# Two transformer layers on one core: the table that fixes every engine's order is laid out in stretches, with eight weightings of TensorE's kinds of jobs tried for each

## What is computed

```python
x = x + attn0(layernorm(x))   # one head, keys and values of 64, causal, with biases
x = x + ffn0(layernorm(x))    # x and weight rounded to fp8, fp16 product, plus bias
x = x + attn1(layernorm(x))   # 16 heads of 16, rotary positions, causal, output projection
x = x + ffn1(layernorm(x))    # mixes each row with the row before it, then
                              # sigmoid(xr @ W_r.T) * (square(relu(xk @ W_k.T)) @ W_v.T)
```

## Time and profile before

| what | value |
|---|---|
| median of three executions | 2672.41 us |
| the profiled execution's own time | 2668.14 us |
| its span, first to last instruction | 2666.3 us |
| TensorE matmuls (PE) busy | 2458.1 us, 92% |
| VectorE (DVE) busy | 1994.6 us, 75% |
| ScalarE (ACT) busy | 1555.9 us, 58% |
| GpSimd (POOL) busy | 597.0 us, 22% |
| mean granted TensorE clock | 0.973 |
| DMA | 159.33 MB, mean 60 GB/s |

### The profile page before, as it was taken

The page is one execution under the profiler, slowest core; times in us unless marked ns, Lnnn a source line. Parts: engine busy times, 40 slices in busy tenths (PEclk is TensorE's granted clock), DMA queues, the critical chain, the costliest instruction groups (busy, mean ns, idle before and its releaser), DMA issues.

```text
span 2666.3 us, 57570 instructions
## 1 busy us (share of the span) xinstructions
PE 2458.1 (92%) x21618; PEld 1123.5 (42%) x21618; DVE 1994.6 (75%) x4256; ACT 1555.9 (58%) x2785; POOL 597.0 (22%) x584
## 2 busy tenths in 40 slices
PE   6888799999999999999999999999989999999996
PEld 4544233444444343453443534343344533433344
DVE  4768788887867878777877778878776788797812
ACT  2335366665645666665655656656655567676662
POOL 5563120213043030222204213030313300000011
PEclk8999799999999999999999999999999999999998
DMA  2323231212212122030302313012130222111110
GB/s 61 103 83 97 67 84 29 67 50 57 78 37 81 49 72 73 26 107 22 96 26 65 97 43 95 20 49 80 40 89 25 72 60 65 39 52 38 29 42 26
DMA packets 225600, 159.33 MB, mean 60 GB/s; under 512 B 91824, under 2 KB 225072, under 8 KB 225328
## 3 DMA queue, kind: packets, MB, share of 16 engines
q1 hardware_dynamic: 224560, 154.75, 20.7%
q10 hardware_dynamic: 768, 0.92, 0.1%
HBM read 87.36 MB, written 67.63 MB: 58 GB/s over the span
## 4 chain that ended last, share of the span: by engine, by line
PE 62%; DVE 21%; ACT 6%; issue 4%; SPq 3%; DMA 1%; POOL 1%; DVEq 1%; POOLq 0%; ACTq 0%
DVE mx L1424 13%; PE psum L1726 13%; PE psum L1703 12%; PE psum L1674 6%; PE psum L1640 4%; ACT probs L1198 3%; PE psum L1514 2%; PE psum L1757 2%; PE psum L1604 2%; PE psum L1575 2%; PE psum L1765 2%; PE psum L1777 2%; PE psum L1746 2%; PE psum L1661 2%; SPq L854 2%
## 5 line engine op out<-in xcount | busy, mean ns | idle before, releaser
L1198 ACT ACTIVATE probs<-psum 128x512 f32<-128x512 f32 x2176 | 1143.8, 605 | 594.6 <-PE psum L1703 380.8
L1424 DVE TENSOR_REDUCE mx<-psum 128x1 f32<-128x512 f32 (+2 forms) x2304 | 1288.6, 623 | 221.4 <-PE psum L1674 165.7
L1703 PE MATMUL psum<-qst,kst 34*128 34x512 bf16 (+7 forms) x5120 | 665.9, 350 | 61.1 <-ACT probs L1198 24.1
L1726 PE MATMUL psum<-probs,vs 128*17 128x512 f32 (+3 forms) x5120 | 585.3, 539 | 0.4
L1674 PE MATMUL psum<-kst,qst 64*128 64x512 bf16 (+3 forms) x2560 | 435.7, 353 | 59.8 <-DVE mx L1424 21.9
L1703 PEld LDWEIGHTS psum<-qst,kst 64*128 64x128 bf16 (+1 forms) x5120 | 190.9, 94 | 412.4 <-ACT probs L1198 134.0
L1674 PEld LDWEIGHTS psum<-kst,qst 64*128 64x128 bf16 x2560 | 132.2, 94 | 371.6 <-ACT probs L1198 136.0
L1726 PEld LDWEIGHTS psum<-probs,vs 128*17 128x17 f32 x5120 | 93.2, 96 | 182.8 <-issue 154.0
L992 POOL TENSOR_SCALAR vare<-mv 128x4 f32<-128x4 f32 x64 | 15.3, 240 | 631.0 <-DVE mv L1300 631.0
L1681 PE MATMUL psum<-maskq,identh 64*128 64x64 bf16 (+1 forms) x2048 | 126.8, 204 | 0.0
L1148 ACT ACTIVATE probs<-psum 128x1024 f32<-128x1024 f32 x80 | 74.6, 940 | 83.3 <-PE psum L1581 49.4
(11 more groups left out here) (160 smaller groups left out, 2847.2 us busy)
## 6 DMA issues: line engine op xcount, KB each, us to landing
qk_dram<-parts SPq DMA_DIRECT2D x224, 128.0 KB
qst<-qk_dram SPq DMA_DIRECT2D x384, 64.0 KB, 2.1
kst<-qk_dram SPq DMA_DIRECT2D x384, 64.0 KB, 2.0
v_dram<-vst SPq DMA_DIRECT2D x64, 136.0 KB, 3.9
vs<-v_dram SPq DMA_DIRECT2D x64, 136.0 KB, 2.2
xs<-x_in SPq DMA_DIRECT2D x16, 512.0 KB, 3.9
x_dram<-xs SPq DMA_DIRECT2D x16, 512.0 KB, 2.9
att_dram<-ast SPq DMA_DIRECT2D x64, 128.0 KB, 2.0
```

The lines of the kernel that those rows point to most:

```text
L1198: act.activation(dst, src, ACT.Exp, scale=DK1 ** -0.5).then_inc(S["exp"], 1)
L1424: ins = dve.tensor_reduce(mx1[:, n % 2, 2 * g + odd, tile % TPC, c:c + 1], bank(src, at, at + cols), AX.X, ALU.max)
L1703: ins = pe.matmul(two[odd][:, at:at + cols], kst[rows, kslot, part, pair, keys], qst[rows, qslot, part, pair, CH - cols:CH], start=(part = ...
L1726: ins = pe.matmul(bank(7, off, CH, rows=VW, row=32 * h), vtile[:, h, :], probs[:, HG * (step_no(b, hg, k) % 2) + h, at:at + CH - off], sta ...
```

## The change

Keys, assumed durations, job lists and everything that builds instructions stay as they are. Only the way in which `run` picks the order changes. It now works in stretches of 40 (assumed us). At the start of each stretch it copies the state and follows eight ways for two stretches (80): way 0 has no weights, the other seven add to the key of every TensorE job a random weight between -10 and +10 that depends on its kind (turn, max, scores, values and so on; the random numbers are seeded, so that the table is the same each time). The way with the least TensorE time that isn't work (waiting and changes of mode) at the end of the two stretches wins, the real state is taken one stretch further with it, and the next eight are tried from there. The sets of jobs and of instructions are the same, in another order, and the banks are dealt out anew. Since the file grows by 51 lines above the instructions, L1674 is L1725 in the changed kernel, L1703 is L1754, and so on.

```diff
@@ -188,12 +188,41 @@
 PATIENCE = 0.25
 
+STRETCH, WAYS, MOVE = 40.0, 8, 10.0
...
+class State:
+    def __init__(self, left, listed, jobs):
...
+        self.now, self.mode, self.todo, self.work = 0.0, None, len(listed), 0.0
+
+    def copy(self):
...
@@ -225,19 +254,39 @@
-        todo = len(self.listed)
...
+        state = State(left, self.listed, jobs)
+        at = 0
+        while state.todo:
+            best = None
+            for way in range(WAYS):
+                weights = self.weights(at, way)
+                trial = state.copy()
+                self.go(trial, then, number, (at + 2) * STRETCH, weights)
+                rank = (max(trial.free_at["PE"], (at + 2) * STRETCH) - trial.work, way)
+                if best is None or rank < best[0]:
+                    best = (rank, weights)
+            at += 1
+            self.go(state, then, number, at * STRETCH, best[1])
+
+    def weights(self, at, way):
+        kinds = sorted({name[0] for name in self.listed if self.jobs[name][0] == "PE"})
+        if way == 0:
+            return {}
+        by = np.random.RandomState(WAYS * at + way).uniform(-MOVE, MOVE, len(kinds))
+        return dict(zip(kinds, by))
...
-        while todo:
+        while todo and now < until:
...
-                    rank = (jobs[name][1] - (STICK if jobs[name][7] == mode and e == "PE" else 0.0), number[name])
+                    rank = (jobs[name][1] - (STICK if jobs[name][7] == mode and e == "PE" else 0.0) + weights.get(name[0], 0.0),
+                            number[name])
...
                 start = now
+                if e == "PE":
+                    state.work += time
```

More of the change, by code:

```diff
@@ L196 @@
 scored, paired = [], []
+class State:
+    def __init__(self, left, listed, jobs):
+        self.left = left
+        self.ready = {e: [] for e in ("PE", "DVE", "ACT", "POOL", "SP")}
+        for name in listed:
+            if not left[name]:
+                self.ready[jobs[name][0]].append(name)
+        self.ready_at = dict.fromkeys(listed, 0.0)
+        self.free_at = dict.fromkeys(self.ready, 0.0)
+        self.order = {e: [] for e in self.ready}
+        self.vacant = [0.0] * 8
+        self.home, self.tenants, self.start = {}, {}, {}
+        self.now, self.mode, self.todo, self.work = 0.0, None, len(listed), 0.0
+    def copy(self):
+        new = State({}, (), {})
+        new.now, new.mode, new.todo, new.work = self.now, self.mode, self.todo, self.work
+        new.left, new.ready_at, new.free_at = dict(self.left), dict(self.ready_at), dict(self.free_at)
+        new.home, new.start, new.vacant = dict(self.home), dict(self.start), list(self.vacant)
+        new.ready = {e: list(names) for e, names in self.ready.items()}
+        new.order = {e: list(names) for e, names in self.order.items()}
+        new.tenants = {n: list(names) for n, names in self.tenants.items()}
+        return new
 class Order:
@@ L227, in run, with go @@
                 then.setdefault(a, []).append(name)
-        ready = {e: [] for e in ("PE", "DVE", "ACT", "POOL", "SP")}
         number = {name: n for n, name in enumerate(self.listed)}
[L230 to L240, removed]
+        state = State(left, self.listed, jobs)
[11 more added lines that the diff above has]
+            self.go(state, then, number, at * STRETCH, best[1])
+        self.home, self.tenants, self.total, self.start = state.home, state.tenants, max(state.free_at.values()), state.start
+        return state.order
+    def weights(self, at, way):
[4 more added lines that the diff above has]
+        return dict(zip(kinds, by))
+    def go(self, state, then, number, until, weights):
+        jobs = self.jobs
+        ready, ready_at, free_at, left = state.ready, state.ready_at, state.free_at, state.left
+        vacant, home, tenants, order = state.vacant, state.home, state.tenants, state.order
+        now, mode, todo = state.now, state.mode, state.todo
         def possible(name):
@@ L294, in run @@
                     mode = md
-                self.start[name] = start
+                state.start[name] = start
                 end = start + time
@@ L312, in run @@
                 now = max(now, nxt)
-        self.home, self.tenants, self.total = home, tenants, max(free_at.values())
-        return order
+        state.now, state.mode, state.todo = now, mode, todo
 def chunk_jobs(o, b, q):
```

## The result

The changed kernel took 2636.98 us (median of four executions, 2634.82 to 2646.92) against 2670.36 us before (2666.52 to 2672.87): a ratio of 0.988 with a 95% interval of 0.9862 to 0.9898, or 33 us less. The forecast was 2656 us, with a range from 2640 to 2683.

What follows compares the result with a forecast made beforehand. TensorE bounds the kernel, busy 2458.1 of 2666.3 us. Terms -8.0 - 5.8 - 2.6 - 3.0 + 4.9 = -14.5 us give 2653.6 from the profiled 2668.1, set at 2656 us towards the median; range 2640 to 2683.

Steps and rivals of the forecast that it cites:

- the clock: Half-clock time of TensorE, seen after two waits at 280 to 290 us: left unchanged, 0, bounds 10 us either way.
- place 1: Third RT to first max at 274.26 us: less work covers the chain, +4.9 us; idle 8 to 9 us as sign.
- The idle time of the middle: TensorE's idle time from 400 to 2533 us: some 16 us less than 112.6, near 96.
- the three terms: Middle: -8.0 us from 7.7% fewer bank and other unexplained waits, -5.8 for one nmaxT wait, -2.6 for load q.
- 42 turnmax with little cover: Of 64 turnmax, 42 now have under 4 us of work since their last max, against 27; no price given.
- Place 2: At 1956 us, TensorE's 5.78 us wait for the bank freed by nmaxT, behind two res, goes: -5.8 us.
- Query slots: First max of block (3, 0, 3) waits 2.56 us for load q; more work now lies between: -2.6 us.
- the two terms: From 117 to 400 us: -3.0 us as 7.7% of 38.4 us idle, and +4.9 us for the less covered chain.
- Start and end: First 64 and last 16 jobs are the same, so 30.6 and most of 23.4 us idle stay: 0.
- Waits that only change places: Rival: a gap closed at one place opens at the next; 2665 to 2672 us, chance 0.28.
- Blocking by res at new places: Rival: res waiting for a put blocks VectorE's list at new places, 5.8 us each; slower, chance 0.14.
- The better packing: Rival: the long stretch comes half way to its best, -25 us instead of -8.0; 2637 to 2641 us, chance 0.10.

Runs made afterwards that it cites:

- run 4: 137 extra matmuls with overwritten results in front of ten long TensorE waits, against the changed kernel; 2626.07 us, ratio 0.9831 to the kernel before.
- run 6: Kernel before with only VectorE's copy nmaxT of block (2, 3, 2) moved in front of the two res; 2670.95 us, ratio 1.0002.
- 9: Kernel before with extra overwritten matmuls in front of its long waits, without the 22 at max (2, 3, 12, 0, 1); 2658.14 us, ratio 0.9956.
- 12: The search with 64 weightings per stretch, plus 47 extra overwritten matmuls in front of four waits of the end; 2605.11 us, ratio 0.9757.
- 64-way list: The changed kernel's search with 64 weightings for each stretch instead of 8, rec doubled; 2610.81 us, ratio 0.9777.

## Why the prediction was wrong in size

**The step that failed is the clock**, "so I leave the clock as it is: 0, bounds 10 us either way". It was -15.3 us in PE busy. Half-clock time went from 78.5 to 51.2 us in the first 400 us and from 41.0 to 17.1 in the middle, and rose from 26.0 to 33.0 in the last 100. These are the sums of TensorE's work while the granted clock was at the half level, before and now (the length of these stretches, then the busy time of each engine in them):

```profile
sum 143.44, PE 107.39 PEld 56.68 DVE 80.52 ACT 33.62 POOL 19.82; mean PE 4.67 PEld 2.46 DVE 3.50 ACT 1.46 POOL 0.86
sum 99.19, PE 71.41 PEld 43.03 DVE 49.86 ACT 28.64 POOL 14.98; mean PE 3.97 PEld 2.39 DVE 2.77 ACT 1.59 POOL 0.83
```

TensorE worked 36.0 us less at that level. If half of such work is the price of the clock, PE busy without it is 2458.1 - 53.7 = 2404.4 us before and 2442.8 - 35.7 = 2407.1 now. So the clock accounts for the whole fall of PE busy (an estimate from these rows).

I had seen one long stretch of it, tied it to place 1, found that place 1 stays, and stopped. That stretch begins at 270.1 us before, as the first of the two waits begins, and at 261.3 us now, ahead of all waits at the place, and lasts 20.5 us in both; with extra matmuls in these waits (run 4) it lasts 3.4. The short ones are many and lie behind other waits. In the middle the trace of before has nine dips of the clock; seven of them come with a wait of TensorE above 1.5 us, at 1113, 1549, 1751, 1819, 1962, 2141 and 2528 us. The changed kernel has five, four of them with such a wait, at 1049, 1311, 2106 and 2275 us.

**Part of this is luck.** The middle has eight waits above 1.5 us before and eight now. Seven of eight brought a dip before, four of eight now, and what decides it isn't shown. In the first 117 us, where both kernels have the same jobs on TensorE, half-clock time is 27.3 us before and 17.1 now; run 6, with TensorE's list as before, has 17.1 too. Twice the share missing from the mean clock, times the span, gives 128 to 155 us over 43 executions of the kernel before (mean 141) and 100 to 132 us over the four of the changed kernel (mean 108). So the change took away about 33 us of half clock rather than the 44.3 of the two profiles.

**What it is worth in time** is less than half its length, since slow matmuls beside a wait cost little (run 4 between 269 and 442 us). Runs 4, 9 and 12 took half-clock time away with the order unchanged and got a fifth to a quarter of it back. Executions of one and the same kernel agree: over 117 executions of 14 kernels, 1 us more at the half level goes with 0.29 us more time (a correlation, in which a long wait could also be the cause of both). At 0.2 to 0.3, 33 to 44 us are 7 to 13 us. The other 20 to 26 of the 33 us then belong to the order itself, for which the sum had 14.5; the idle time of the profile fell by 17.2 only, perhaps because faster matmuls beside a wait leave more of it idle. Where these further 6 to 12 us lie stays open.

**The idle time of the middle** was forecast near 96 us and is 95.8. The sum of the three terms for it, -8.0 - 5.8 - 2.6 = -16.4, met the 16.8 us measured. In this stretch alone the four bank rows add up to 19.6 + 14.5 + 12.9 + 6.8 = 53.8 us before and 11.1 + 14.3 + 11.8 + 8.9 = 46.1 now, 7.7 us less, where 7.7% of 53.8 gave 4.1. I named the other side, 42 turnmax with little cover instead of 27, and gave it no price. TensorE's wait for the folded maxima in the middle, before and now:

```profile
PE psum L1686 <- DVE nmaxb L1441: 11.7, 12, 2.7
PE psum L1737 <- DVE nmaxb L1492: 16.6, 19, 2.0
```

It cost 4.9 us, but turnmax's wait for VectorE's mx fell from 5.5 to 1.6 us, so that little cover cost about 1 us in all. Of the 8.3 us by which the row of the whole trace grew, most is the one wait of 6.1 us at place 1.

**Place 2**, -5.8 us: the wait is gone from the list of the changed kernel (0.6 us in two waits are left). The step's reason was half wrong. Run 6 shows that moving res away from the copy does nothing while the next max still takes the bank that RT holds. It is the new banks (2 and 5) and the earlier RT that could free it. "Next late would be the max's own operands" was an assumption that I should have read from the tenants of both banks.

**Query slots**, -2.6 us: 8.6 us in 3 waits became 0.9 in one. Right, and more, since place 1's part is in it.

**Place 1**, +4.9 us: the chain from RT to load q isn't what TensorE waits for first, and it was not fixed either: from the start of the third RT to the issue of load q there are 8.1 us now (259.70 to 267.77) against 9.8 in the earlier trace rows. One wait of before belongs to the place as well, the changed kernel's rows stand below it:

```profile
268.11 0.22 PE L1686 MATMUL psum<-identb,nmaxb 128*32 128x128 bf16 x1 [1.23 <-DVE nmaxb L1441]
```

```profile
269.31 0.26 PE L1737 MATMUL psum<-identb,nmaxb 128*32 128x128 bf16 x1 [6.14 <-DVE nmaxb L1492]
271.33 1.94 PE L1565 MATMUL psum<-ident,xn 128*128 128x128 f32 x8 [1.76 <-DVE xn L1370]
273.21 1.04 PE L1725 MATMUL psum<-kst,qst 64*128 64x512 bf16 x4
278.45 1.89 PE L1754 MATMUL psum<-qst,kst 64*128 64x512 bf16 x8 [4.21 <-DMA qst<-nmaxT]
```

12.1 us of waiting (6.14 + 1.76 + 4.21) where the earlier trace rows and the 1.23 us ahead of them had 11.1. Turnmax waits for VectorE, which does two res, eight norm instructions and then, after 1.67 us without a visible wait, the folded maxima. Under that wait and the turn behind it load q lands, and the first max doesn't wait at all, where I expected 8 to 9 us as a sign. The shorter cover cost 1 us, not 4.9, and from 117 to 400 us idle time fell by 1.6 us (38.4 to 36.8) where the two terms had +1.9.

**Start and end**, 0: the first jobs are the same, but the last 66 us hold 27.1 us of idle time instead of 23.4, since the turn of the last chunk but one now stands behind the last values jobs and no longer ahead of them: TensorE waits 2.67 and 4.10 us for VectorE there, before 2.29.

**The rivals.** Waits that only change places: no, in the change. Blocking by res at new places: TensorE's longest wait for VectorE's resid is 2.2 us and for its nmaxT 0.3 us. The better packing, with 0.10, had the right time for another reason: it put all of 31.5 us into gaps, and the gaps gave 17.2.

**And the draw.** Three draws of the same search with eight ways give 2637, 2643 and 2669 us, 1.2, 1.0 and 0.1% under the kernel before. The change has the best of the three, and neither the diff nor the profile of before could tell that. The table ranks them 2621, 2617 and 2630. The poorest comes last in both, but the first two change places.

## What to carry to other kernels

A search over orders that counts the waits of the bounding engine in a table of assumed times worked here, with tables 13 to 50 us shorter than the profiled times. What the chip gives back can be double the table's gain, or nothing: try several draws and widths on the chip, and keep the measured best. When waits of TensorE go, price the clock too, from the half-clock time of the whole trace and not from its longest stretch, and from several executions, since it swings by 27 us in one kernel. And before a wait is put down to the one that ended it, look at everything that the waiting job needs, each of its banks by itself.

## What the runs showed that I had not expected

Extra matmuls whose results are thrown away made both kernels faster when they ran inside waits for data: 11 us with 137 of them in the changed kernel, 13 us with 128 in the one before, about 6 us with 47 in the 64-way list. Behind a wait for a bank 22 of them took 6.80 us for themselves. The Trainium skill, page "TensorE: Matmul & The Clock Gate", section "Loop structure matters more than you think", says that a long wait on a DMA between matmuls lets TensorE go cold, while VectorE's copy out of PSUM, with the next matmuls right behind, doesn't. The first part is as in these traces: the changed kernel waits 3.31 us for a DMA up to 1311 us, and 3.4 us at the half clock begin at 1312.6. VectorE's work is harmless only while matmuls go on: in the last 66 us no DMA is waited for at the four groups shown, TensorE waits 2.67 and 5.59 us for VectorE's xn and 4.10 us for its xrk, and the groups behind run at the half clock, 6.67 us instead of 3.72.
